# A graph network layer: P is gathered in two exact parts and added to Q by TensorE, ScalarE copies z out, its sums are products with itself, and the degrees move to a later stage

## What is computed

```
messages = relu(batchnorm(concat(node_rep[src], edge_rep[dst]) @ W1))   # over 50000 edges
edge_new = segment_sum(messages, dst)
aggregate = segment_sum(edge_new[dst], src)
h = (1 + epsilon) * node_rep + aggregate
```

## Time and profile before

| | us |
|---|---|
| median of 3 timed runs | 3554.77 |
| lowest, highest | 3550.27, 3555.87 |
| span of the profiled execution, first to last instruction | 3565.2 |

### The profile page before, as it was taken

The page is one execution under the profiler, slowest core; times in us unless marked ns, Lnnn a source line. Parts: engine busy times, 40 slices in busy tenths (PEclk is TensorE's granted clock), DMA queues, the critical chain, the costliest instruction groups (busy, mean ns, idle before and its releaser), DMA issues. The chain is left out here.

```text
span 3565.2 us, 41686 instructions
## 1 busy us (share of the span) xinstructions
PE 2424.9 (68%) x12339; PEld 1976.6 (55%) x12339; DVE 2395.4 (67%) x4693; ACT 1352.5 (38%) x2800; POOL 1734.6 (49%) x1269
## 2 busy tenths in 40 slices
PE   4668733454555543666621999879999999925998
PEld 3522213454444443444421897469888988923788
DVE  5979945777777778877886544344565566615788
ACT  2268833444444441000000435424434434423776
POOL 0257887776667667888888777730000000042000
PEclk9779865555555555888855999889999999966999
DMA  9993224665555656555533774146545645340355
GB/s 373 351 355 34 22 26 130 174 171 164 165 165 166 172 170 137 133 142 134 143 40 39 202 177 89 1 103 185 175 126 172 185 130 173 118 103 8 109 173 176
DMA packets 338453, 517.84 MB, mean 145 GB/s; under 512 B 145379, under 2 KB 227100, under 8 KB 331580
## 3 DMA queue, kind: packets, MB, share of 16 engines
q1 hardware_dynamic: 190254, 436.41, 38.2%
q0 software_dynamic: 134768, 58.41, 14.2%
q10 hardware_dynamic: 13214, 20.35, 1.7%
HBM read 369.65 MB, written 145.38 MB: 144 GB/s over the span
## 5 line engine op out<-in xcount | busy, mean ns | idle before, releaser
L1133 PE MATMUL banks<-rows_r,lhs_r 128*128 128x448 f32 x3500 | 899.1, 372 | 84.0 <-issue 41.6
L728 POOL DMA_INDIRECT counts<-wts x391 | 637.4, 1630 | 307.9 <-DMA counts<-ring 141.0
L1133 PEld LDWEIGHTS banks<-rows_r,lhs_r 128*128 128x128 f32 x3500 | 667.8, 191 | 152.9 <-issue 74.8
L741 POOL DMA_INDIRECT weights<-wts x391 | 620.9, 1588 | 161.8 <-issue 159.1
L1133 PE MATMUL banks<-ring_r,lhs_r 128*128 128x448 f32 x1750 | 525.8, 370 | 0.0
L749 POOL DMA_INDIRECT reg<-tab_p,w x416 | 406.9, 978 | 217.9 <-issue 122.8
L548 DVE SCALAR_TENSOR_TENSOR ring_r<-ring,dinv,rows_r 128x896 fp32r<-128x896 f32 (+1 forms) x300 | 303.7, 1033 | 309.5 <-ACT rows_r L535 309.3
L1221 PE MATMUL banks<-lhs_r,oT 128*128 x416 | 203.3, 489 | 429.8 <-issue 346.6
L535 ACT ACTIVATE rows_r<-ring,dinv 128x896 fp32r<-128x896 f32 (+1 forms) x300 | 285.0, 951 | 399.3 <-PE banks L1133 342.0
L799 POOL DMA_INDIRECT el<-tab_l,base_i x25 | 24.0, 958 | 796.8 <-DMA tab_l<-reg 789.5
L1221 PEld LDWEIGHTS banks<-lhs_r,oT 128*128 128x128 f32 x416 | 131.9, 317 | 447.3 <-issue 447.0
(11 more groups left out here) (269 smaller groups left out, 4104.6 us busy)
## 6 DMA issues: line engine op xcount, KB each, us to landing
ring<-weights SPq DMA_DIRECT2D x225, 448.0 KB
ring<-counts SPq DMA_DIRECT2D x150, 448.0 KB
zbuf<-reg SPq DMA_DIRECT2D x208, 256.0 KB
reg<-zbuf SPq DMA_DIRECT2D x52, 1024.0 KB
counts<-ring SPq DMA_DIRECT2D x25, 1568.0 KB, 16.4
weights<-ring SPq DMA_DIRECT2D x25, 1568.0 KB
ring<-weights SPq DMA_DIRECT2D x75, 224.0 KB
dr<-low_rows_d SPq DMA_DIRECT2D x52, 256.0 KB
```

Source lines behind the costliest of these rows:

```text
L728: pool.indirect_dma_start(counts, bass.IndirectOffsetOnAxis(ap=ix_c[:, k:k + 1], axis=0), vals_c[:, k:k + 1], None, compute_op=ALU.add).th ...
L741: pool.indirect_dma_start(weights, bass.IndirectOffsetOnAxis(ap=ix_w[:, k:k + 1], axis=0), vals_w[:, k:k + 1], None, compute_op=ALU.add).t ...
L1133: m = pe.matmul(bank[:, 0:BLK], lhs[part], rows[:, c:c + BLK], start=first, stop=last)
```

## The change

The change has six parts.

1. P is split into `p_high` (rounded to float32r) and `p_low` (the rest, also exact) in four parts of up to 7 node tiles; ACT rounds, DVE subtracts, and ACT's queue stores both next to each other. A row of `tab_p` is now 2 KB, and a gather moves 256 KB in place of 128 KB.
2. PE adds the gathered rows: two float32r matmuls of 512 columns with an identity matrix, into the bank that also takes Q. POOL's gathers wait for PE (`zq_done`) in place of DVE. ACT copies z out of PSUM. DVE's `add_z` is gone.
3. The sums: for each tile and each half of the channels one float32 matmul of 130 columns of z (with two columns of ones) by z itself. The diagonal is the sum of squares. DVE's `sum_z` and ACT's squares are gone. The batch norm's vectors are now columns (2 values a partition) and PE spreads the bound row over the partitions.
4. The degrees (ACT, DVE, PE) stand in the message stage, and so do the DVE operations that turn them into `dinv`. ACT clears `en` and `en_odd` in place of DVE.
5. A pass has one load of 8 tile numbers in place of 8 loads, on PE in the z stage and on DVE in the message stage.
6. POOL adds one column of counts after every eighth gather in place of every fourth, so 52 in the z stage in place of 104. `W_MID` is (4,)*15 + (3,), so 126 weights go between the later counts in place of 140, and 14 pair tests are made in place of 13.

```diff
-C_PER = 1
-W_FROM, W_PER, W_MID = 42, 7, (7, 7, 4, 3, 7)
+C_EVERY = 8
+W_FROM, W_PER, W_MID = 42, 7, (4,) * 15 + (3,)
...
-        tab_p = nc.dram_tensor("tab_p", (NP, H), F32).ap()
+        tab_p = nc.dram_tensor("tab_p", (NP, 2 * H), F32).ap()
...
+        def load_tiles(eng, regs, i):
+            eng.load(regs, tile_ix[0:1, 8 * i:8 * i + 8])
+            return [eng.snap(r, min_val=0, max_val=NT - 1) for r in regs]
...
                 if k >= 8 and k % 2 == 0:
-                    pool.wait_ge(z_ready, (k - 8) // 2 + 1)
+                    pool.wait_ge(zq_done, (k - 8) // 2 + 1)
...
                 gather(k)
-                if k % 4 == 3:
-                    add_counts(C_PER)
+                if k % C_EVERY == C_EVERY - 1:
+                    add_counts(1)
...
-            act.dma_start(nat(tab_p), g_nat[:, 0:NT - 1, :]).then_inc(tables_stored, 16)
...
+            for k, ts in enumerate(p_parts):
+                n = len(ts)
+                if k >= 2:
+                    act.wait_ge(p_stored[k % 2], 16 * (k // 2))
+                    act.wait_ge(p_low_ready, k - 1)
+                act.activation(p_high_r[k % 2][:, 0:n * H].rearrange("p (t c) -> p t c", c=H),
+                               g_nat[:, ts[0]:ts[-1] + 1, :], ACT.Copy).then_inc(p_high_ready, 1)
+                act.wait_ge(p_high_ready, k + 1)
+                store_rows(p_high[k % 2][:, 0:n, :], ts[0], 0, p_stored[k % 2])
+            act.wait_ge(p_low_ready, len(p_parts))
+            store_rows(lhs_split(0, 0).bitcast(F32), 0, 1, tables_stored)
...
-                    act.wait_ge(z_ready, q + 1)
-                    act.activation(zsq[q % SQ], zz[q % ZS], ACT.Square).then_inc(sq_ready, 1)
...
+                    act.wait_ge(zq_done, q + 1)
...
+                    if q >= ZS:
+                        act.wait_ge(z_stored[q // 2 % (ZS // 2)], 32 * (q // ZS))
+                        act.wait_ge(z_acc, q - ZS + 1)
+                    act.activation(z_rows(q), ps[4 + q % 2].rearrange("p (a c) -> p a c", c=H), ACT.Copy).then_inc(z_ready, 1)
...
+                for k in (2 * q, 2 * q + 1):
+                    pe.wait_ge(gathered[k % 8], 16 * (k // 8 + 1))
+                bank, s = ps[4 + q % 2], 2 * q % 8
+                for part in range(2):
+                    pe.matmul(bank[:, 0:2 * H], ident_r[:, :], gp_rows[:, s:s + 2, part * H:(part + 1) * H],
+                              start=part == 0, stop=False, skip_group_check=True)
...
+            def square_sums(q):
+
+                pe.wait_ge(z_ready, q + 1)
+                for k in range(2):
+                    for j in range(JH):
+                        o = 2 + k * (H + 2) + j * P
+                        a = o - 2 if j == 0 else o
+                        m = pe.matmul(stat_bank[j][:, 0:P + 2], zz[q % ZS][:, o:o + P], zz[q % ZS][:, a:a + P + 2],
+                                      start=(q == 0 and k == 0), stop=(q == KQ - 1 and k == 1))
+                m.then_inc(z_acc, 1)
...
                     m.then_inc(m_sum, 1)
+                    if i < NBAT:
+                        degrees(2 * q)
+                        degrees(2 * q + 1)
...
+            for k, ts in enumerate(p_parts):
+                tiles_k = slice(ts[0], ts[-1] + 1)
+                v.wait_ge(p_high_ready, k + 1)
+                v.tensor_tensor(lhs_split(0, 0)[:, tiles_k, :], g_nat[:, tiles_k, :], p_high[k % 2][:, 0:len(ts), :],
+                                ALU.subtract).then_inc(p_low_ready, 1)
...
-                v.tensor_tensor(zz[q % ZS], ps[4 + q % 2],
-                                gp[:, k:k + 2, :].rearrange("p a c -> p (a c)"), ALU.add).then_inc(z_ready, 1)
...
-                v.tensor_tensor(zacc2, zacc2, z_both(q), ALU.add).then_inc(z_acc, 1)
```

More of the change, by code:

```diff
@@ L480, in tiles_of @@
             return range(key[-1] * per, min(NT, key[-1] * per + per))
+        p_parts = [range(a, min(NT, a + P_PART)) for a in range(0, NT, P_PART)]
         passes = ["agg0", "agg10", "agg11", "agg12", "agg3"]
@@ L901, in _, with store_rows @@
             act.wait_ge(centred, 1)
[L902 to L904 removed]
+            def store_rows(got, t0, part, s):
+                cs = slice(part * H, (part + 1) * H)
+                end = t0 + got.shape[1]
+                full = min(end, NT - 1)
+                act.dma_start(tab_p[t0 * P:full * P, cs].rearrange("(t p) c -> p t c", p=P),
+                              got[:, 0:full - t0, :]).then_inc(s, 16)
+                if end == NT:
+                    o, k = full * P, full - t0
+                    act.dma_start(tab_p[o:o + 48, cs], got[0:48, k, :]).then_inc(s, 16)
+                    act.dma_start(tab_p[o + 48:N, cs], got[48:LAST, k, :]).then_inc(s, 16)
+            for k, ts in enumerate(p_parts):
[9 more added lines that the diff above has]
+            store_rows(lhs_split(0, 0).bitcast(F32), 0, 1, tables_stored)
             load_cells(4)
@@ L1209, in _ @@
             q_lo = q_low[:, :].rearrange("p (t c) -> p t c", c=H)
+            gp_rows = gp_r[:, :].rearrange("p (k c) -> p k c", c=2 * H)
             tiles = [None] * KS
+            pe_regs = [pe.alloc_register(f"pe_tile{k}") for k in range(8)]
             def add_q(q):
@@ L1235, in _ @@
                     add_q(q)
-                    if i and i <= NBAT:
-                        degrees(2 * q - 8)
-                        degrees(2 * q - 7)
+                    if q >= 2:
+                        square_sums(q - 2)
                     if q - 2 in TESTED:
                         group_totals(TESTED[q - 2])
+            square_sums(KQ - 2)
+            square_sums(KQ - 1)
             for q in (KQ - 2, KQ - 1):
@@ L1243, in _ @@
                     group_totals(TESTED[q])
-            pe.wait_ge(z_acc, KQ + 1)
-            for part in range(2):
-                for k in range(2):
-                    o = (2 * part + k) * H
-                    m = pe.matmul(stat_bank[:, part * H:(part + 1) * H], ones[:, :], zsum[:, o:o + H], start=(k == 0), stop=(k == 1))
-            m.then_inc(stat_done, 1)
-            pe.wait_ge(abs_a, 1)
+            pe.wait_ge(nb_ready, 1)
             for j in range(JH):
-                m = pe.transpose(ps[5][:, j * P:(j + 1) * P], absg[:, j * P:(j + 1) * P], ident[:, :])
-            m.then_inc(a_cols, 1)
+                m = pe.matmul(nb_ps[:, j * P:(j + 1) * P], bn_c[:, 7, j:j + 1].to_broadcast([P, P]), ident[:, :], start=True, stop=True)
+            m.then_inc(nb_rows, 1)
             for i in range(NPASS):
@@ L1475, in _ @@
             equal_group(0)
-            v.wait_ge(g_loaded, 48)
+            v.wait_ge(g_loaded, 64)
             sign = scan[0][:, 0:H]
@@ L1662, in _ @@
-            v.wait_ge(a_cols, 1)
-            do(v.tensor_scalar(neg_a[:, :], ps[5][:, 0:H].rearrange("p (j c) -> p j c", j=JH)[:, :, 0], -1.0, None, ALU.mult))
+            v.wait_ge(z_acc, KQ)
+            mean_c, sq_c, var_c, std_c, a_c, ra_c, bt_c, nb_c = (bn_c[:, k, :] for k in range(8))
+            for j in range(JH):
+                o = 2 if j == 0 else 0
+                v.tensor_tensor(diag_t[:, j, :], stat_bank[j][:, o:o + P], ident[:, :], ALU.mult)
+                last = v.tensor_scalar(mean_c[:, j:j + 1], stat_bank[j][:, 0:1] if j == 0 else stat_bank[j][:, P:P + 1], 1.0 / E, None, ALU.mult)
@@ new lines, in _ @@
+            do(last)
+            do(v.tensor_reduce(sq_c, diag_t, AX_X, ALU.add))
+            do(v.tensor_tensor(var_c, mean_c, mean_c, ALU.mult))
+            do(v.scalar_tensor_tensor(var_c, sq_c, 1.0 / E, var_c, ALU.mult, ALU.subtract))
+            do(max_zero(var_c))
+            v.tensor_scalar(var_c, var_c, BN_EPS, None, ALU.add).then_inc(bn_var, 1)
+            do(v.tensor_scalar(bt_c, g_col[:, :], 0.0, None, ALU.is_ge))
+            do(v.tensor_scalar(bt_c, bt_c, 2.0, -1.0, ALU.mult, ALU.add))
@@ L1676, in messages @@
                                 ALU.max).then_inc(msg_ready, 1)
+            v_regs = [v.alloc_register(f"v_tile{k}") for k in range(8)]
             destinations(0)
+            v.wait_ge(nb_rows, 1)
+            do(v.tensor_copy(nb_row[:, :], nb_ps))
             messages(0)
+            v.wait_ge(en_cleared, 2)
+            degree_rows(0)
             for i in range(NPASS):
@@ L1683, in _ @@
                     messages(i + 1)
-                tiles = [v.value_load(tile_ix[0:1, k:k + 1], min_val=0, max_val=NT - 1) for k in range(8 * i, 8 * i + 8)]
+                if i + 1 < NBAT:
+                    degree_rows(i + 1)
+                tiles = load_tiles(v, v_regs, i)
                 for k in range(8 * i, 8 * i + 8):
```

164 lines of the change are left out of this document (79 added, 85 removed).

## The result

The changed kernel takes 3608.76 us (median of 4 runs, 3605.5 to 3615.32) and the kernel before 3553.53 us beside it: ratio 1.0161, with a 95% interval of 1.014 to 1.0182. It is slower by 55 us, where I forecast 64 us less.

The account below looks back on a forecast made before the run. POOL's time before 2356 us was taken to bound the kernel. Front +13, z stage -179, last gather to last count +82 and behind it +20 gave -64 us, from 3554.8 to 3491 us; range 3465 to 3552.

Parts of the forecast that it names:

- with 0.2 us a pass for small waits, 52 x 12.4 = 645 us: z stage: POOL stays the bound at 12.4 us a pass, 645 us instead of 824, a gain of 179 us.
- the stall starts on PE: z stage: PE stands still 9.49 us around 8 tile-number loads, starving DVE and POOL; 93 us of stalls.
- From the last gather to the last count: +82 us: POOL between those points: 42 more adds at 1.85 us, +78, and 4 us for adds lengthened by DVE neighbours.
- Front: +13 us: Before the gathers: more stored bytes delay group 4's cells to about 224 us, making POOL 13 us late.
- the slower bound: Front: 33 us for storing another 3.2 MB, where 24 us was taken; POOL's lateness then at most 22 us.
- Behind the last count: +20 us: POOL beside the first dense pass: 10 more weight adds there, at 1.85 to 2.15 us each.
- Rival 1: z stage: DMA engines bound it at 281 GB/s, 13.1 us a pass, 3527 us in all; chance 24%.
- Rival 2: z stage: PE bounds it at the low clock, 16.0 us a pass, 3678 us in all; chance 12%.
- Rivals 3 and 4: Message stage late from added degree work, up to 3550 us, 6%; gather price growing with bytes, 3583 us, 4%.
- the point at which the gain is gone: z stage: a us more per pass costs 52, so a pass of 13.6 us cancels the 64 us gain.
- the forecast's range: Whole kernel: 3470 us (12.2 us a pass, 9 us in front, no longer adds) to 3517 us; chance 54%.
- rival 3: Message stage: PE's and DVE's degree work makes it late, 3500 us at 9.5 us a pass, 3550 at 10.5; 6%.

Follow-up runs that it names:

- the third group: Runs sharing a chip: kernel before again, changed kernel again, kernel before with only the counts and W_MID part, kernel before with one load; kernel before took 3456.1 us.
- the long groups: First and fourth groups of runs, where the unchanged kernel before took 3554.6 and 3572.9 us.
- ten slots: Changed kernel with 10 slots for gathered rows in place of 8 and 6 buffers for z in place of 8; ratios 1.015 and 1.0111.
- the short group: A group where the unchanged kernel before took 3455.3, 3456.1 or 3458.1 us (second, third, fifth); here the third.
- the fourth group: Runs on more slots, some with other edits, and the changed kernel again; the kernel before took 3572.9 us.
- the long run: The kernel before, unchanged, in its first profiled execution; span 3565.2 us.
- before again: The kernel before, unchanged, run once more in the third group; 3458.4 us.
- Three banks: Changed kernel with three PSUM banks for z in place of two, square sums three pairs behind; ratio 1.0176, run in a short group only.
- the square sums: Changed kernel with the square sums of one tile of each pair left out, except first and last pair; ratio 1.015, second group.
- aligned rounds: Changed kernel with W_MID = (4, 3) * 7 + (7, 7), so each group of 7 weights begins a round; ratio 1.0048, 3571.1 us.
- the cells first: Changed kernel with the cells of group 4 loaded ahead of the store of P's low part; ratio 1.0135, 3504.3 us.
- the second group: Runs of the changed kernel on more slots, fewer square sums and earlier cells; the kernel before took 3455.3 us.

## Why the prediction was wrong, point by point

**The step that failed: "with 0.2 us a pass for small waits, 52 x 12.4 = 645 us".** Under it lay "the stall starts on PE", at the eight loads. That reading rested on one pass boundary and on the releaser column of the earlier trace rows, which names the engine that POOL waits for, not why that engine is late. The runs of the third group take it apart: with the same loads, and pauses up to the same 10.1 us, the kernel before has no stall. In the long groups a stall of 78 to 95 us stands in the changed kernel, which has one load, and with half the bytes and ten slots too. In the profiled execution it cost 707 us in place of 645, 63 of the 108 us by which the sum was off.

What the runs showed in place of that cause is a signal between engines that arrives late. In the long groups it can be seen at ScalarE. Its waits before the copy of z, in the changed kernel of the result, and then in that of the third group:

```profile
ACT reg L973 <- remote: 287.4, 51, 9.4
ACT reg L973 <- PE banks L1281: 252.7, 80, 65.0
```

```profile
ACT reg L973 <- PE banks L1281: 570.5, 203, 63.4
```

"Remote" is a wait whose end the profile can't put down to any instruction. In the short group there is none. One of the long ones in the changed kernel of the result, on PE's timeline and on ACT's:

```profile
917.25 0.28 PE L1281 MATMUL banks<-q_low,oT 128*128 x1
...
919.09 0.28 PE L1281 MATMUL banks<-q_low,oT 128*128 x1
```

```profile
921.11 1.09 ACT L973 ACTIVATE reg<-banks 128x512 f32<-128x512 f32 x2 [5.48 <-remote]
```

Two pairs have their last product at 917.25 and 919.09 us, and both are copied from 921.11 us on, the first 3.6 us after its product's end. ScalarE also waits for an earlier store of z at this place, so this alone could be a late store. But POOL's next gather for a slot in use, the 209th, waits for nothing except the first of the two products, and it starts later still:

```profile
921.86 0.98 POOL L770 DMA_INDIRECT gp_r<-tab_p,w  x1 [1.87 <-remote]
```

The whole stage says the same. I take from a trace each gather that starts over 0.3 us later than the usual gap of 0.30 us, and the time from the end of the product that it waits for to its start. In the changed kernel of the third group there are 20 such gathers (17 us of stalls), and the time is 0.79 us for each of them. In that of the result there are 55 (79 us), and the median is 4.3 us; in the fourth group with ten slots 61 (90 us), and the median is 5.6 us. So most of this stall is neither PE's work nor the transfers: the product is done, and POOL is told late.

In the kernel before, POOL follows DVE's add after 0.79 us in the long run too. There DVE itself is late. Its waits before the add, z stage of the long run; before again has no such row:

```profile
DVE reg L1599 <- remote: 103.2, 27, 11.0
```

What holds the signals back, in some groups and not in others, I could not settle. It isn't the bytes of the gathers, the number of slots or the eight loads alone. Three banks, and the square sums in a long group, are open.

**With the stall out of the way the mechanism was right and the conclusion still wrong.** In the third group the z pass is 12.39 us (forecast 12.4), the gather 0.968 us (0.98), and PE's clock 0.87 (above 0.7). But the kernel before has 14.08 us a pass there, so the stage gives back 88 us and not 179. POOL's 1198 instructions are the same before and after. What leaves the z stage comes back behind it (-100, +78 and +20 us), so the change can be worth only the stalls that it takes away, less the waits that it adds. I had both halves in the sum and did not draw this line under it.

**"From the last gather to the last count: +82 us"** was too small by 27. The adds cost what I took. The 31 us of waits inside the rounds of four I did not see: I had counted the weights of `W_MID` and not laid its rounds against the groups of 7 in `add_weight`. The run with aligned rounds shows them. The stage was not late for DVE's sake: the last count set its end.

**"Front: +13 us"** was too small by 9. The cells came 30.6 us late in place of 22.6, near the slower bound, and the later groups did not catch up. With the cells first the front is 14 us late.

**"Behind the last count: +20 us"** measured 24 and 17 us. The 5 us behind the last weight are a small part that I had at nothing.

**The rivals.** Rival 1 gave 13.1 us a pass, near the 13.60 measured, but for a wrong reason: with half the bytes the pass stays, and in the second group the run with ten slots carried 301 GB/s without one stall, above the 281 GB/s that I had scaled for a full share. Its z stage in a window, and below it that of the changed kernel in the third group:

```profile
566.00:1194.00 628.00, 474.58 (x3764) 437.03 (x3764) 227.86 (x790) 121.98 (x204) 485.91 (x467) 0.89 0.96 301
```

```profile
564.00:1208.00 644.00, 486.82 (x3764) 448.66 (x3764) 227.52 (x790) 121.85 (x204) 484.13 (x467) 0.87 0.94 294
```

By the rule of the Trainium skill (DMA: Bandwidth & Descriptors, Anatomy of one DMA), which is stated for a single transfer, I had estimated 8.5 us for the bytes of a pass; the second row gives 0.94 of 12.39 us, 11.6 us of busy engines a pass. So the estimate is too low for this mix of transfers. That the bytes do not bind, as it had said, the run with ten slots bears out. Rival 2 is out: PE is busy 73% of the z stage at a clock of 0.85. With the rule of the Trainium skill (TensorE: Matmul & The Clock Gate, The HAM clock gate) that activity releases the half rate, the trace agrees: 0.50 became 0.85 to 0.87. Rivals 3 and 4 are out too: the pair tests end at 1818.5 us, 146 us ahead of the last count, and a gather costs the same. I had put the point at which the gain is gone at 13.6 us a pass. The pass was just that, and the 45 us of the other four terms made it slower. Two sums in the prediction are also off by some us, and no chance hangs on them: by its own terms the lower end of the forecast's range is 3473 us and not 3470, and rival 3 comes to 3502 and 3554 us, not 3500 and 3550.

**A version that beats both kernels** is the kernel before with one load of tile numbers: 0.9914 where before is long, 1.0007 (no difference) where it is short. The best of the PE version, with ten slots, part 6 taken back and the cells first, has 0.9937 in a long group. In the short groups no run was faster than before, but the changed kernel with part 6 taken back ran in long groups alone.

## What to carry to other kernels

When one engine's queue bounds several stages, work moved from one to the other along it is worth nothing. Count only the stalls that go and the waits that come, and lay each rhythm in the code (rounds of 4, groups of 7) against the waits that it meets. Before you count a stall as gone, look at what the engine that is named as its releaser waits for, and check that cause over all passes and not at one boundary: a pause that coincides with a stall need not be its cause. Compare too when the awaited instruction ended with when the waiting one started: here that split a late signal from slow work. A trace is one execution of one group of runs; run the kernel before again beside the experiments.

## What was not expected of the hardware

The kernel before took 3455 to 3458 us in three groups and 3554 to 3573 us in the others, the third and the fourth on the same chip. In the traces 91 of the 108 us between the spans of 3565.2 and 3456.7 us are POOL's stalls of the z stage, and 20 lie behind the last weight (1210.8 and 1191.0 us); an add or a gather costs the same. In the short groups' stalls POOL starts 0.79 us after the end of PE's product, in the long ones 4 us and more at the median. The DMA engines carried 301 GB/s at a share of 0.96 under gathers, stores and loads at once. A gather of 128 rows costs POOL 0.97 us for 1 KB and for 2 KB a row.
